# Transposing the residual by DMA instead of on TensorE, in a graph network with an LSTM

## The chip, the cores and the metric

The kernel runs on one core of a Trainium2 chip. The metric is device microseconds of that core for one execution, as the median of three runs.

## The reference

The input x has 32 batches of 256 nodes with 128 features. Four layers follow each other, each with a residual: `x = layernorm(x + layer(x))`. Layer 0 is a gated neighbour sum over the matrix adj. Layer 1 is a normalised neighbour sum, two dense layers (128 to 256 to 128), each with a batch norm over all 32 x 256 rows. Layer 2 is attention over the 256 nodes of a batch. Layer 3 is two neighbour sums with dense layers and then, for window lengths p = 1 to 4, an LSTM that runs p steps over windows of the nodes and writes its last state back. Cut to what matters here:

```python
x = _layernorm(x + _L0_gnn_ref(x, adj, ...), axis=-1)
x = _layernorm(x + _L1_gnn_ref(x, adj, ...), axis=-1)   # out = batchnorm(h @ W2.T + b2)
x = _layernorm(x + _L2_gnn_ref(x, adj, ...), axis=-1)
x = _layernorm(x + _L3_gnn_ref(x, adj, ...), axis=-1)
```

## The kernel before

The batches go in 8 groups of 4 (`GB`), so a group is 1024 rows of 128 features: 8 tiles of 128 x 128 (`TILES`; `COLS` = 1024). Everything is float32. Each engine has its own instruction queue, written out by hand, and the engines meet by semaphores.

The batch norms of layer 1 need all groups, so the kernel has two parts. The first does layer 0 and layer 1's matmuls for all groups. It leaves X1 (the sum after layer 0, normalised, with nodes on the partitions) and O2T (layer 1's output before its last batch norm, with features on the partitions) in SBUF. The second part goes in turns, `slot(s)` on each engine, for s = 2 to 10. In turn s four groups are in work at once: group s in stage A (end of layer 1, layer 2), group s - 1 in stage B (the matmuls of layer 3), group s - 2 in stage L (11 LSTM steps, `NSTEP`), group s - 3 in stage T (the last layernorm and the output). Groups 0 and 1 go through stage A ahead of the turns, in an order of their own. Stage A exists in turns 2 to 7, six times.

**The residual.** At the start of stage A the sum X1 + O2 is wanted with nodes on the partitions, and O2T has features there. GpSimd first scales and shifts O2T by the batch norm, two groups ahead (`scaled(s + 2)`, L504, semaphore yt_ok). TensorE then makes eight transposes into the PSUM tensor PA (`a_residual`, L680). VectorE adds X1 and writes Z (`a_sum1`, L1552, semaphore z1_ok). From Z come the row statistics (`a_norm1`, L1400), the dot products with two vectors (`a_dots`, L1570, 16 instructions, then `a_s12`, L1576) and ScalarE's normalised X2 (`norm_apply`, L1042).

**TensorE's order in a turn** is x(0), a_residual(s), x(1), t_turn, a_spread0 for two batches, x(2), a_spread0 for the other two, x(3), h(3), a_rows, a_weigh0, x(4), and on to step 10 with the attention's matmuls in between. x(k) and h(k) are the input and state matmuls of LSTM step k (L831, L843). The four gates have a PSUM bank each (`QQ`), so gate q of step k + 1 waits until ScalarE's tanh (L1200) has read gate q of step k.

**VectorE's order** is inner(0), a_sum1, state(0), inner(1), a_small2(s - 1), state(1), a_norm1, cell(2), t_sum (L1779), a_dots, a_s12, cell(3), a_max, cell(4) and so on. inner(k) (L1680, L1726 and others) makes the cell state, state(k) (L1708) the hidden state, cell(k) is both. x(2) waits for state(1), x(4) for state(3).

**GpSimd's order** in a turn is `rstd(1, 0, s)` (L446, L452), `scaled(s + 2)`, `tail(s - 3)` (L446 and L525, after step 6), then `rstd` and `scale2(s)` (L446, L512) for the two halves of group s. a_spread0(s) in the next turn waits for scale2. **SP's queue** has only DMAs: the loads, then the eight stores of a group's output as they become ready.

Of SBUF, the quarter `late[:, 2]` (2048 words of a partition) holds nothing in the turns.

Of the kernel before, what the change touches and what calls it, by code (L numbers as in the profile page):

```python
# [19 lines left out]

F32 = mybir.dt.float32
ACT = mybir.ActivationFunctionType
AX = mybir.AxisListType

P = 128
# [75 lines left out]
def build(nc, x, xt, adj, early_in, later_in, lstm_w, out):  # L101
    ctx = ExitStack()
    with ctx:
# [3 lines left out]
        def sem(name):  # L107
            return ctx.enter_context(nc.semaphore(name))
# [13 lines left out]
        MS, E1 = (late[:, k, :].rearrange("p (t n) -> p t n", n=NODES) for k in range(2))  # L122
        HS = late[:, 3, 0:2 * BANK].rearrange("p (k n) -> p k n", k=2)
        ZF = late[:, 3, 2 * BANK:4 * BANK]

        AN = late[:, 0, 0:BANK].rearrange("p (c n) -> p c n", c=NC)
        DIAG = late[:, 2, 0:NC * P].rearrange("p (c n) -> p c n", c=NC)
# [245 lines left out]
                  + [(i, h) for i in range(AHEAD, NCHUNK) for h in range(HC)])  # L373

        half_ps = sem("half_ps")

        lanes = [Lane(g_ps, g_ok, ca_ok, cf_ok, cell_ok, tc_ok, h_ok, Q, NGATE * LAST + GATE_AT[LANED, I],
                      FORGETS[NSTEP] * LAST, NSTEP * LAST + LANED),
# [13 lines left out]
        @block.sync  # L392
        def _(sp):
            def load_xt(g):
                sp.dma_start(XT[:, g % NX], xt[g]).then_inc(xt_in[g % NX], 16)

            def load_x(g):
                sp.dma_start(XIN[:, g % NX], x[g]).then_inc(x_in[g % NX], 16)

            sp.dma_start(AD[:, 1], adj[:, 1]).then_inc(adjt_in, 16)  # L400
            load_x(0)
            sp.dma_start(early[:], early_in).then_inc(early_ok, 16)
            load_xt(0)
            sp.dma_start(AD[:, 0], adj[:, 0]).then_inc(adj_in, 16)
            load_x(1)
            load_xt(1)
            load_x(2)
            load_xt(2)
            sp.dma_start(later[:], later_in).then_inc(later_ok, 16)
            load_xt(3)  # L410
            load_x(3)
            for g in range(NX, GROUPS):
                sp.wait_ge(gate_ps, g - NX + 1)
                load_xt(g)
                sp.wait_ge(mix3, g - NX + 1)
                load_x(g)
            sp.dma_start(WT[:], lstm_w).then_inc(lstm_in, 16)

            for g in range(GROUPS - 1):
                sp.wait_ge(ln[3]["out"], TILES * (g + 1))  # L420
                sp.dma_start(out[g], OUT[:, g % 2]).then_inc(sent[g % 2], 16)
            half = TILES // 2 * P
            sp.wait_ge(last_act, TILES // 2)
            sp.dma_start(out[GROUPS - 1][:, 0:half], OUT[:, 1, 0:half]).then_inc(sent[1], 16)
            sp.wait_ge(last_dve, LAST_DVE)
            sp.wait_ge(last_act, TILES - LAST_DVE)
            sp.dma_start(out[GROUPS - 1][:, half:], OUT[:, 1, half:]).then_inc(sent[1], 16)
            sp.wait_ge(sent[0], 16 * (GROUPS // 2))
            sp.wait_ge(sent[1], 16 * (GROUPS // 2 + 1))
# [3 lines left out]
        def _(pool):  # L433
# [66 lines left out]
            def scaled(g):  # L500
# [2 lines left out]
                o2 = O2T[:, g * COLS:(g + 1) * COLS]  # L503
                pool.tensor_scalar(o2, o2, BN[:, 4, 0:1], BN[:, 5, 0:1], ALU.mult, ALU.add).then_inc(yt_ok, 1)  # L504

            def scale2(g, h=None):
                f = front(g)
                pool.wait_ge(ln[2]["rstd"], halves(g, h))
# [19 lines left out]
            def slot(s, par, A, B, L, T):  # L528
                if A:
                    rstd(1, 0, s)  # L530
                    scaled(s + 2)
                if T:
                    tail(s - 3, 1 - par)
                if A:
                    for h in range(2):
                        rstd(2, 1, s, h)
                        scale2(s, h)
# [5 lines left out]
            rstd(1, 2, 1, 1)  # L543
            scaled(2)
            scaled(3)
            rstd(2, 1, 0, 0)
            scale2(0, 0)
            rstd(2, 1, 0, 1)
# [1 line left out]
            rstd(2, 2, 1, 0)  # L550
            rstd(2, 2, 1, 1)
            scale2(1)
            slots(slot)


        @block.tensor
        def _(pe):
# [113 lines left out]
                output1(i, h)  # L671


            def a_residual(g, h=None):
                pe.wait_ge(half_ok, 1) if (g, h) == (0, 1) else pe.wait_ge(yt_ok, g + 1)
                reach(pe, z2_ok, TILES * before(g))
                for b in batches(h):
                    for c in range(NC):
                        at = g * COLS + b * NODES + c * P
                        mm = pe.transpose(turned(front(g).PA, c, b), O2T[:, at:at + P], ident[:])  # L680
                mm.then_inc(y_ps, size(h))


            def a_preload(g, h):
                bs = slice(2 * h, 2 * h + 2)
                pe.matmul(front(g).PA[:, part(h)].rearrange("p (b c d) -> p b c d", c=NC, d=P), ident[:],
# [92 lines left out]


            def a_spread0(g, some, h=None):
                reach(pe, z1_ok, 2 * upto(g + 2) - 4)
                for b in some:
                    pe.wait_ge(ln[2]["out"], TILES * g + NC * (b + 1))
                    for m in range(NC):
# [109 lines left out]
            def slot(s, par, A, B, L, T):  # L895
# [47 lines left out]
                        h(k) if STEPS[k][1] else None  # L943
                    return
                x(0)
                a_residual(s) if A else None
                x(1)
                t_turn(s - 3, 1 - par) if T else None
                a_spread0(s - 1, (0, 1)) if B else None
# [391 lines left out]
        def _(dve):  # L1341
# [203 lines left out]
            o2 = O2T[:, 0:BANK]  # L1545
            dve.tensor_scalar(o2, o2, BN[:, 4, 0:1], BN[:, 5, 0:1], ALU.mult, ALU.add).then_inc(yt_ok, 1)

            def a_sum1(g, h=None):
                dve.wait_ge(y_ps, halves(g, h))
                f = front(g)  # L1550
                bs = slice(batches(h)[0], batches(h)[-1] + 1)
                dve.tensor_tensor(f.Z[:, part(h)].rearrange("p (b c d) -> p b c d", c=NC, d=P),  # L1552
                                  f.PA[:, part(h)].rearrange("p (b c d) -> p b c d", c=NC, d=P),
                                  X1[:, g, :].rearrange("p (c b d) -> p b c d", c=NC, d=P)[:, bs], ALU.add).then_inc(z1_ok, size(h))

            def a_norm1(g, h=None):
                if g < 2:
# [396 lines left out]
```

## Time and profile before

| what | us |
|---|---|
| median of 3 runs (lowest, highest) | 638.43 (638.06, 638.8) |
| span of the profiled execution | 636.4 |
| median of the runs less that span | 2.0 |
| TensorE busy, matmuls (share of the span) | 621.6 (98%) |
| VectorE busy | 474.8 (75%) |
| ScalarE busy | 433.8 (68%) |
| GpSimd busy | 167.4 (26%) |
| turns 2 to 7, start to start | 57.4 to 57.7 each |

The profile is of one execution. Its span runs from the first to the last instruction; no other time is recorded for that execution, so a sum is made against the span and carried to the runs with the 2.0 us between. PE is TensorE's matmul, PEld its weight load, DVE is VectorE, ACT is ScalarE, POOL is GpSimd, SP issues DMAs. L504 is line 504 of the kernel before. The rows name tensors by the first name of their memory: `HB` is also O2T, `raw` the LSTM's gates and cells, `four` the input, Z2 and output buffers, `one_a` to `one_d` work buffers.

### The profile page before, as it was taken

Reading aid. Unit: us, or ns where it says so; the run is one execution under the profiler, and the core shown is the slowest. Engines: PE = TensorE matmul, PEld = TensorE weight load, DVE = VectorE, ACT = ScalarE, POOL = GpSimd, SP = SyncE. Lnnn points to the kernel's source line nnn. Section 1 sums busy time; section 2 is a strip of 40 time slices with the busy share of each in tenths; the row PEclk is TensorE's granted clock in tenths of the full one; section 3 lists DMA queues with packets and bytes.
Section 4 is the critical chain, followed back from the end, with each engine's and each line's share of the span. In section 5 each row is a group of like instructions: output and inputs, shape, how many; then the busy total and the mean of one; then the engine's idle time right before and its main releaser. Section 6 shows DMA issues by size and latency. Waiting matters only on the chain.

```text
span 636.4 us, 9580 instructions
## 1 busy us (share of the span) xinstructions
PE 621.6 (98%) x2768; PEld 440.9 (69%) x2768; DVE 474.8 (75%) x1623; ACT 433.8 (68%) x995; POOL 167.4 (26%) x228
## 2 busy tenths in 40 slices
PE   9999999999999999999999999999999999999994
PEld 6756656447975687578658757865885687577794
DVE  4999999876847767866887787688768767465656
ACT  3667767966947766795677577557847766546774
POOL 1464551005233002304503240341143032103211
PEclk9999999999999999999999999999999999999998
DMA  8424000000000000000000000000000000000000
GB/s 337 142 115 166 1 1 1 1 0 2 2 1 1 0 2 0 2 2 33 2 0 2 34 1 2 33 2 1 1 33 2 2 28 6 1 1 33 2 35 33
DMA packets 4372, 16.84 MB, mean 26 GB/s; under 512 B 480, under 2 KB 480, under 8 KB 4192
## 3 DMA queue, kind: packets, MB, share of 16 engines
q1 hardware_dynamic: 4320, 16.23, 6.6%
q8 instruction: 22, 0.36, 0.2%
q14 instruction: 30, 0.25, 0.1%
HBM read 12.03 MB, written 4.19 MB: 26 GB/s over the span
## 4 chain that ended last, share of the span: by engine, by line
PE 76%; DVE 3%; ACT 2%; issue 1%; POOL 0%; POOLq 0%; ACTq 0%; DVEq 0%
PE QQ L831 26%; PE QQ L843 15%; PE PA L814 4%; PE PA L786 4%; PE PB L805 2%; PE PB L796 2%; PE PB L667 2%; PE PA L667 2%; PE PA L767 2%; PE PB L767 2%; PE QQ L865 1%; PE PB L884 1%; PE PB L746 1%; PE PA L746 1%; PE QQ L875 1%
## 5 line engine op out<-in xcount | busy, mean ns | idle before, releaser
L1200 ACT ACTIVATE raw<-QQ,BL 128x256 f32<-128x256 f32 (+2 forms) x279 | 150.1, 558 | 75.1 <-PE QQ L843 37.7
L831 PE MATMUL QQ<-HT,WT 128*128 128x256 f32 (+2 forms) x558 | 183.9, 474 | 1.1 <-ACT raw L1200 0.6
L446 POOL TENSOR_TENSOR RSD<-VAR,pw 128x4 f32<-128x4 f32 (+1 forms) x43 | 61.8, 1438 | 381.7 <-DVE VAR L1422 381.7
L831 PEld LDWEIGHTS QQ<-HT,WT 128*128 128x128 f32 x558 | 103.5, 190 | 59.2 <-issue 28.3
L843 PE MATMUL QQ<-HB,WT 128*128 128x256 f32 (+2 forms) x336 | 100.2, 441 | 0.4 <-DVE HB L1708 0.2
L843 PEld LDWEIGHTS QQ<-HB,WT 128*128 128x128 f32 x336 | 61.2, 190 | 29.3 <-issue 13.4
L1236 ACT ACTIVATE raw<-raw 128x256 f32<-128x256 f32 (+4 forms) x79 | 37.1, 470 | 25.9 <-DVE raw L1690 19.7
L1680 DVE SCALAR_TENSOR_TENSOR raw<-raw 128x256 f32<-128x256 f32 (+2 forms) x60 | 32.5, 542 | 20.2 <-ACT raw L1200 19.6
L1708 DVE SCALAR_TENSOR_TENSOR HB<-raw 128x256 f32<-128x256 f32 (+4 forms) x42 | 20.1, 478 | 23.5 <-ACT raw L1236 23.5
L1042 ACT ACTIVATE X<-Z,OFF,RSD 128x128 f32<-128x128 f32 x80 | 31.8, 482 | 2.0 <-POOL OFF L452 2.0
L512 POOL TENSOR_SCALAR X<-four,MEAN,RSD 128x128 f32<-128x128 f32 x64 | 30.7, 494 | 1.6
L622 PE MATMUL PA<-AHT,X 128*128 128x256 f32 x128 | 29.5, 384 | 1.5 <-ACT X L1042 1.3
L1163 ACT ACTIVATE HB<-HB,EB 128x256 f32<-128x256 f32 x64 | 30.9, 500 | 0.2
L786 PE MATMUL PA<-AD,X 128*128 128x256 f32 x128 | 30.3, 379 | 0.0
L622 PEld LDWEIGHTS PA<-AHT,X 128*128 128x128 f32 x128 | 23.7, 190 | 9.5 <-issue 6.3
L525 POOL TENSOR_SCALAR four<-HB,MEAN,RSD 128x128 f32<-128x128 f32 x56 | 29.7, 544 | 0.7
L636 PE MATMUL QQ<-one_b,later 128*128 128x512 f32 x64 | 29.1, 598 | 0.2 <-ACT one_b L1071 0.2
L814 PE MATMUL PA<-AD,Y 128*128 128x256 f32 x128 | 29.2, 380 | 0.0
L786 PEld LDWEIGHTS PA<-AD,X 128*128 128x128 f32 x128 | 23.9, 191 | 6.8 <-issue 4.1
L814 PEld LDWEIGHTS PA<-AD,Y 128*128 128x128 f32 x128 | 24.2, 190 | 4.2
L1083 ACT ACTIVATE HB<-QQ 128x512 f32<-128x512 f32 x32 | 17.9, 586 | 12.8 <-PE QQ L636 12.5
L599 PE MATMUL PB<-four,AD 128*128 128x512 f32 x56 | 25.7, 601 | 0.4 <-DMA four<-in_x 0.4
(249 smaller groups left out, 1177.5 us busy)
## 6 DMA issues: line engine op xcount, KB each, us to landing
four<-in_x SPq DMA_DIRECT2D x8, 512.0 KB, 4.0
raw<-in_xt SPq DMA_DIRECT2D x8, 512.0 KB, 6.5
out<-four SPq DMA_DIRECT2D x7, 512.0 KB, 2.6
WT<-in_lstm SPq DMA_DIRECT2D x1, 2048.0 KB, 8.0
later<-in_later SPq DMA_DIRECT2D x1, 725.5 KB, 10.3
AD<-in_adj SPq DMA_DIRECT2D x2, 256.0 KB, 4.8
out<-four SPq DMA_DIRECT2D x2, 256.0 KB, 2.0
early<-in_early SPq DMA_DIRECT2D x1, 275.0 KB, 4.5
```

What stands on the lines that cost most here:

```text
L446: pool.tensor_tensor(RSD[kk][:, ts], VAR[kk][:, ts], pw[:, ts], ALU.pow).then_inc(ln[k]["rstd"], some)
L512: pool.tensor_scalar(tile_of(X1, g, c, b), nth(f.Z2, t), MEAN[f.kk2][:, t:t + 1], RSD[f.kk2][:, t:t + 1], ALU.add, ALU.mult).then_inc(ln[2 ...
L622: mm = pe.matmul(PA[:, b * NODES:(b + 1) * NODES], tile_of(X1, g, m, b), AHT[:, m, :], start=(m == 0), stop=(m == NC - 1))
L786: mm = pe.matmul(PA[:, b * NODES:(b + 1) * NODES], tile_of(X1, g, m, b), ADJT[:, m, :], start=(m == 0), stop=(m == NC - 1))
L814: mm = pe.matmul(PA[:, b * NODES:(b + 1) * NODES], turned(Y, m, b), ADJT[:, m, :], start=(m == 0), stop=(m == NC - 1))
L831: mm = pe.matmul(steps_view(Q[q], k), WT[:, 0, (p - 1) * 4 + q, :], ht_view(par, k), start=True, stop=(s == 0))
L843: pe.matmul(Q[q][:, 0:nw * GB], WT[:, 1, (p - 1) * 4 + q, :], HS[:, (k - 1) % 2, 0:nw * GB], start=False, stop=True).then_inc(g_ps, 1)
L1042: act.activation(nth(to, t), nth(z, t), ACT.Identity, bias=OFF[kk][:, t:t + 1], scale=RSD[kk][:, t:t + 1]).then_inc(ln[k]["out"], 1)
L1163: e = act.activation(f.E1[:, t], f.E1[:, t], ACT.Exp, bias=f.EB[:, t:t + 1], scale=1.0, accum_out=DEN[:, t:t + 1] if g > 1 else None)
L1200: act.activation(TG[q][:, at:n], Q[q][:, at:n], ACT.Tanh, scale=0.5 if q == G else 0.25, bias=BL[:, p - 1, q:q + 1]).then_inc(g_ok, 1)
L1236: act.activation(TC[:, at:n], CELL[:, at:n], ACT.Tanh, scale=0.5).then_inc(tc_ok, 1)
L1680: dve.scalar_tensor_tensor(out=target[:, 0:n], in0=TG[I][:, 0:n], scalar=1.0, in1=TG[G][:, 0:n], op0=ALU.add, op1=ALU.mult).then_inc(cell_ ...
```

## The change

The eight transposes on TensorE go. In their place GpSimd, a turn ahead, copies group s + 1 of O2T, seen as 16-bit half-words, into two planes (low halves, high halves; `split`). SP issues one DMA transpose of the 128 x 2048 half-words, in 16 blocks of 128 columns (`turn_residual`). GpSimd weaves the two turned planes back into float32 words in Z (`merge`). VectorE's add then reads Z and X1 from SBUF and writes Z. The planes lie in `late[:, 2]`.

In turn s GpSimd does split(s + 1) and merge(s + 1) between scaled(s + 2) and tail(s - 3), for s = 2 to 6. For group 2, split(2) stands behind scaled(3), ahead of the turns, and merge(2) is GpSimd's last instruction before turn 2. merge(g) waits for the DMA, and for the readers of the Z before it (a_dots and ScalarE's norm_apply of group g - 1). a_spread0's wait for z1_ok becomes one for z2_ok of the group that it works on. Groups 0 and 1 are as before.

```diff
--- before.py
+++ after.py
@@ -19,6 +19,7 @@
 from concourse.alu_op_type import AluOpType as ALU
 
 F32 = mybir.dt.float32
+U16 = mybir.dt.uint16
 ACT = mybir.ActivationFunctionType
 AX = mybir.AxisListType
 
@@ -122,6 +123,7 @@
         MS, E1 = (late[:, k, :].rearrange("p (t n) -> p t n", n=NODES) for k in range(2))
         HS = late[:, 3, 0:2 * BANK].rearrange("p (k n) -> p k n", k=2)
         ZF = late[:, 3, 2 * BANK:4 * BANK]
+        PLAIN, TURNED = (late[:, 2, k * COLS:(k + 1) * COLS].bitcast(U16) for k in range(2))
 
         AN = late[:, 0, 0:BANK].rearrange("p (c n) -> p c n", c=NC)
         DIAG = late[:, 2, 0:NC * P].rearrange("p (c n) -> p c n", c=NC)
@@ -373,6 +375,7 @@
                   + [(i, h) for i in range(AHEAD, NCHUNK) for h in range(HC)])
 
         half_ps = sem("half_ps")
+        split_ok, turned_in, merged_ok = (sem(n) for n in ("split_ok", "turned_in", "merged_ok"))
 
         lanes = [Lane(g_ps, g_ok, ca_ok, cf_ok, cell_ok, tc_ok, h_ok, Q, NGATE * LAST + GATE_AT[LANED, I],
                       FORGETS[NSTEP] * LAST, NSTEP * LAST + LANED),
@@ -416,7 +419,15 @@
                 load_x(g)
             sp.dma_start(WT[:], lstm_w).then_inc(lstm_in, 16)
 
+            def turn_residual(g):
+                sp.wait_ge(split_ok, g - 1)
+                reach(sp, merged_ok, g - 2)
+                sp.dma_start_transpose(TURNED.rearrange("p (k n) -> p k n", n=P), PLAIN).then_inc(turned_in, 16)
+
+            turn_residual(2)
+            turn_residual(3)
             for g in range(GROUPS - 1):
+                turn_residual(g + 4) if g + 4 < GROUPS else None
                 sp.wait_ge(ln[3]["out"], TILES * (g + 1))
                 sp.dma_start(out[g], OUT[:, g % 2]).then_inc(sent[g % 2], 16)
             half = TILES // 2 * P
@@ -503,6 +514,21 @@
                 o2 = O2T[:, g * COLS:(g + 1) * COLS]
                 pool.tensor_scalar(o2, o2, BN[:, 4, 0:1], BN[:, 5, 0:1], ALU.mult, ALU.add).then_inc(yt_ok, 1)
 
+            def split(g):
+
+                pool.wait_ge(yt_ok, g + 1)
+                reach(pool, turned_in, 16 * (g - 2))
+                o2 = O2T[:, g * COLS:(g + 1) * COLS].bitcast(U16)
+                pool.tensor_copy(PLAIN.rearrange("p (k n) -> p k n", k=2), o2.rearrange("p (n k) -> p k n", k=2)).then_inc(split_ok, 1)
+
+            def merge(g):
+
+                pool.wait_ge(turned_in, 16 * (g - 1))
+                if g > 2:
+                    pool.wait_ge(dots_ok, 2 * TILES * (g - 2))
+                    pool.wait_ge(ln[1]["out"], TILES * g)
+                pool.tensor_copy(Z[:].bitcast(U16).rearrange("p (n k) -> p k n", k=2), TURNED.rearrange("p (k n) -> p k n", k=2)).then_inc(merged_ok, 1)
+
             def scale2(g, h=None):
                 f = front(g)
                 pool.wait_ge(ln[2]["rstd"], halves(g, h))
@@ -529,6 +555,8 @@
                 if A:
                     rstd(1, 0, s)
                     scaled(s + 2)
+                    split(s + 1) if s + 1 < GROUPS else None
+                    merge(s + 1) if s + 1 < GROUPS else None
                 if T:
                     tail(s - 3, 1 - par)
                 if A:
@@ -543,6 +571,7 @@
             rstd(1, 2, 1, 1)
             scaled(2)
             scaled(3)
+            split(2)
             rstd(2, 1, 0, 0)
             scale2(0, 0)
             rstd(2, 1, 0, 1)
@@ -550,6 +579,7 @@
             rstd(2, 2, 1, 0)
             rstd(2, 2, 1, 1)
             scale2(1)
+            merge(2)
             slots(slot)
 
 
@@ -671,16 +701,6 @@
                 output1(i, h)
 
 
-            def a_residual(g, h=None):
-                pe.wait_ge(half_ok, 1) if (g, h) == (0, 1) else pe.wait_ge(yt_ok, g + 1)
-                reach(pe, z2_ok, TILES * before(g))
-                for b in batches(h):
-                    for c in range(NC):
-                        at = g * COLS + b * NODES + c * P
-                        mm = pe.transpose(turned(front(g).PA, c, b), O2T[:, at:at + P], ident[:])
-                mm.then_inc(y_ps, size(h))
-
-
             def a_preload(g, h):
                 bs = slice(2 * h, 2 * h + 2)
                 pe.matmul(front(g).PA[:, part(h)].rearrange("p (b c d) -> p b c d", c=NC, d=P), ident[:],
@@ -779,7 +799,7 @@
 
 
             def a_spread0(g, some, h=None):
-                reach(pe, z1_ok, 2 * upto(g + 2) - 4)
+                pe.wait_ge(z2_ok, TILES * (g + 1)) if g else None
                 for b in some:
                     pe.wait_ge(ln[2]["out"], TILES * g + NC * (b + 1))
                     for m in range(NC):
@@ -943,7 +963,6 @@
                         h(k) if STEPS[k][1] else None
                     return
                 x(0)
-                a_residual(s) if A else None
                 x(1)
                 t_turn(s - 3, 1 - par) if T else None
                 a_spread0(s - 1, (0, 1)) if B else None
@@ -1545,13 +1564,10 @@
             o2 = O2T[:, 0:BANK]
             dve.tensor_scalar(o2, o2, BN[:, 4, 0:1], BN[:, 5, 0:1], ALU.mult, ALU.add).then_inc(yt_ok, 1)
 
-            def a_sum1(g, h=None):
-                dve.wait_ge(y_ps, halves(g, h))
-                f = front(g)
-                bs = slice(batches(h)[0], batches(h)[-1] + 1)
-                dve.tensor_tensor(f.Z[:, part(h)].rearrange("p (b c d) -> p b c d", c=NC, d=P),
-                                  f.PA[:, part(h)].rearrange("p (b c d) -> p b c d", c=NC, d=P),
-                                  X1[:, g, :].rearrange("p (c b d) -> p b c d", c=NC, d=P)[:, bs], ALU.add).then_inc(z1_ok, size(h))
+            def a_sum1(g):
+                dve.wait_ge(merged_ok, g - 1)
+                z = Z[:].rearrange("p (b c d) -> p b c d", c=NC, d=P)
+                dve.tensor_tensor(z, z, X1[:, g, :].rearrange("p (c b d) -> p b c d", c=NC, d=P), ALU.add).then_inc(z1_ok, 2)
 
             def a_norm1(g, h=None):
                 if g < 2:
```

## Rows read from the trace of the kernel before

**Rows 1.** Busy time by stretch, turn 4: length, then each engine's busy us and instructions.

```profile
core 0: us, PE busy (x) PEld busy (x) DVE busy (x) ACT busy (x) POOL busy (x), PEclk, DMA share, GB/s
...
302.85:360.34 57.49, 57.49 (x251) 41.45 (x251) 44.08 (x154) 40.38 (x91) 15.69 (x23) 1.00 0.03 10
```

**Rows 2.** Timeline, all engines, start of turn 4: start us, us, what, idle before and releaser.

```profile
304.99 0.42 ACT L1236 ACTIVATE raw<-raw 128x256 f32<-128x256 f32 x1 [2.08 <-DVE raw L1690]
305.26 1.04 PE L680 MATMUL PA<-ident,HB 128*128 128x128 f32 x8
305.32 1.83 ACT L1200 ACTIVATE raw<-QQ,BL 128x512 f32<-128x512 f32 x3
...
306.14 2.32 PE L831 MATMUL QQ<-HT,WT 128*128 128x512 f32 x5
```

**Rows 3.** Timeline, all engines, x(2) of turn 4.

```profile
310.62 0.69 DVE L1708 SCALAR_TENSOR_TENSOR HT<-raw 128x512 f32<-128x512 f32 x1
...
311.36 0.19 PEld L831 LDWEIGHTS QQ<-HT,WT 128*128 128x128 f32 x1 [0.21 <-DVE HT L1708]
```

**Rows 4.** Timeline of GpSimd, turn 4.

```profile
316.78 1.20 POOL L504 TENSOR_SCALAR HB<-HB,BN 128x1024 f32<-128x1024 f32 x1
344.56 1.75 POOL L446 TENSOR_TENSOR RSD<-VAR,pw 128x8 f32<-128x8 f32 x1 [26.59 <-DVE VAR L1422]
...
358.92 1.01 POOL L446 TENSOR_TENSOR RSD<-VAR,pw 128x4 f32<-128x4 f32 x1 [8.30 <-DVE VAR L1422]
```

**Rows 5.** Timeline of VectorE, turn 4, from t_sum to step 3.

```profile
316.31 1.22 DVE L1779 SCALAR_TENSOR_TENSOR HB<-PB,X 128x1024 f32<-128x1024 f32 x1
317.44 0.68 DVE L1570 CUSTOM_DVE_ANT_0 one_a<-Z,WAR 128x128 f32<-128x128 f32 x1
...
318.04 0.28 DVE L1570 CUSTOM_DVE_ANT_0 one_a<-Z,WAR 128x128 f32<-128x128 f32 x1
...
321.84 0.69 DVE L1726 SCALAR_TENSOR_TENSOR raw<-raw 128x512 f32<-128x512 f32 x1 [0.33 <-ACT raw L1200]
```

**Rows 6.** Timeline, all engines, a_dots of turn 2.

```profile
201.72 1.49 POOL L504 TENSOR_SCALAR HB<-HB,BN 128x1024 f32<-128x1024 f32 x1
...
202.24 1.11 DVE L1570 CUSTOM_DVE_ANT_0 one_a<-Z,WAR 128x128 f32<-128x128 f32 x1
```

**Rows 7.** Timeline, all engines, start of turn 2.

```profile
188.72 3.88 POOL L512 TENSOR_SCALAR X<-four,MEAN,RSD 128x128 f32<-128x128 f32 x8
...
191.80 1.23 DVE L1552 TENSOR_TENSOR Z<-PA,X 128x1024 f32<-128x1024 f32 x1 [0.37 <-PE PA L680]
...
194.17 0.69 DVE L1680 SCALAR_TENSOR_TENSOR raw<-raw 128x512 f32<-128x512 f32 x1 [0.55 <-ACT raw L1200]
...
196.37 1.13 PE L831 MATMUL QQ<-HT,WT 128*128 128x512 f32 x2 [0.37 <-DVE HT L1708]
```

**Rows 8.** Groups by line and shape, whole span: busy us, mean ns of one.

```profile
L478 POOL TENSOR_TENSOR one_d<-one_d,Y 128x512 f32<-128x512 f32 x6 | 7.9, 1340 | 10.9 <-ACT one_d L1056 10.9
...
L1452 DVE SCALAR_TENSOR_TENSOR X<-X,four 128x1024 f32<-128x1024 f32 x4 | 4.9, 1224 | 0.1
```

**Rows 9.** Line L504: shortest, median and longest ns, first and last start.

```profile
L504 POOL TENSOR_SCALAR HB<-HB,BN x7: 1193/1195/1492, 145.0 to 374.3; 128x1024 f32<-128x1024 f32 x7
```

**Rows 10.** Timeline of GpSimd, ahead of the turns.

```profile
169.65 1.01 POOL L446 TENSOR_TENSOR RSD<-VAR,pw 128x4 f32<-128x4 f32 x1 [12.93 <-DVE VAR L1422]
```

**Rows 11.** Timeline, all engines, x(4) of turn 4.

```profile
325.02 0.40 PEld L831 LDWEIGHTS QQ<-HT,WT 128*128 128x128 f32 x2 [0.45 <-DVE HT L1708]
...
325.23 0.45 PE L831 MATMUL QQ<-HT,WT 128*128 128x340 f32 x1
```

**Rows 12.** Timeline of VectorE, step 3 in turn 2 and in turn 6.

```profile
206.85 0.69 DVE L1726 SCALAR_TENSOR_TENSOR raw<-raw 128x512 f32<-128x512 f32 x1 [1.15 <-ACT raw L1200]
...
436.83 0.69 DVE L1726 SCALAR_TENSOR_TENSOR raw<-raw 128x512 f32<-128x512 f32 x1 [0.71 <-ACT raw L1200]
```

**Rows 13.** DMA issues: count, KB each, median us from issue to landing.

```profile
out<-four SPq DMA_DIRECT2D x7, 512.0 KB, 2.6
```

## The prediction

> **What bounds the kernel now.** I read the busy time by stretch first. Turns 2 to 7, in which the changed code runs, last about 57.5 us each, and in turn 4 TensorE is busy for all of it [rows 1]. That invites the reading that eight matmuls less are eight matmuls saved. So I went on to the timeline of one turn's start, to see not whether TensorE is busy but what would let it begin the next matmul sooner. In turn 4 the queue is x(0), the residual, x(1), t_turn, half of a_spread0, x(2). x(1) begins at 306.14 [rows 2]. It overwrites the bank of gate I, so it waits for ScalarE's tanh of x(0)'s gate I. That tanh starts at 305.32 in a run of three (1.83 us, about 0.6 each and 0.69 for one alone), so it ends at about 306.0 [rows 2]. It cannot start sooner: before it in ScalarE's order stands the last tanh of the turn before (304.99), which had waited 2.08 us for VectorE [rows 2]. One step on, x(2)'s weights are loaded at 311.36, after a wait on VectorE's L1708, which runs from 310.62 for 0.69 us [rows 3]. So the residual fills a hole: TensorE is full, but the LSTM chain through ScalarE and VectorE arrives at the same moment to within 0.1 us, twice.
>
> Then the two engines that get work. GpSimd is idle for most of a turn: it ends L504 at 317.98 and is wanted again at 344.56 and 358.92 [rows 4]. VectorE is the one to watch, since some of its instructions stop while GpSimd runs [rows 5, 6].
>
> **The change, part by part.**
>
> *Removed: eight transposes a turn.* In turn 4 from 305.26 to 306.14, 0.88 us [rows 2], so 5.3 us in six turns if all of it counted. By the paragraph above x(1) can come up by about 0.1 us and x(2) by less than 0.1. In the five full turns (3 to 7) the gain is 0 to 0.4 us together; I take 0. In turn 2 x(1) would come up by the whole 0.88, but there another wait decides, next.
>
> *VectorE's add.* a_sum1 read PSUM and X1 and now reads Z and X1: 1.23 us before [rows 7], 1.22 for an add of the same size with both inputs in SBUF [rows 8]. No change. Its new wait, merged_ok, is met long before in turns 3 to 7.
>
> *merge(2) ahead of turn 2.* It stands on GpSimd behind scale2(1), eight instructions from 188.72 that end at 192.60 [rows 7]. Before, a_sum1(2) began at 191.80. Now it waits for the whole merge. Behind it on VectorE stand state(0), inner(1) and state(1), for which x(2) waits.
> The price of a copy: no row shows one of 2048 half-words. Nearest is L504, 1024 elements in 1.195 us when undisturbed [rows 9]; an instruction that it locked out (below) lost 0.83 us, which is the part that grows with length, so twice the elements cost 1.195 + 0.83 = 2.05 us. Lower bound: 1.2, if two half-words pass as one word. Upper bound: 5.2, four times the 1.3 us of a two-input operation on 512 elements [rows 8].
> With 2.05 and 0.1 to start, merge ends at 194.75 and a_sum1 starts 3.0 late. inner(1) had 0.55 us of waiting on ScalarE in front of it [rows 7], which absorbs that much: x(2) comes at about 198.8 instead of 196.37, **2.4 us late**, in place of the 0.88 gained. split(2) and its transfer lie earlier, in a gap of GpSimd of 12.9 us before 169.65 [rows 10], and have until 192.6: nothing.
>
> *split in turns 2 to 6.* It runs behind rstd and scaled, while VectorE does a_dots. In turn 2 L504 ran from 201.72 to 203.21, and the a_dots instruction that started at 202.24 took 1.11 us [rows 6] against 0.28 [rows 5]. In turn 4 the first a_dots takes 0.68 and is over when L504 is [rows 4, 5]. L1779, which has one input in PSUM, ran beside L504 in its usual 1.22 [rows 4, 5]. So two-SBUF-input instructions of VectorE stand still while GpSimd streams, 0.83 us for 1024 elements, 1.7 for split's 2048.
> The Trainium skill, "SBUF — State Buffer", section "SBUF: two separate sides", has this as an exclusive lock held for the whole instruction; by that 2.05 would be lost to a copy and not 1.7, and the sum would be some 3 us higher.
> What is late next: a_dots, then L1726 of step 3, which has 0.33 us of slack (its wait on ScalarE) [rows 5], then h for x(4): L1708's release at 325.02, the matmul at 325.23, 0.2 of slack [rows 11]. So x(4) is late by 1.7 - 0.33 - 0.2 = 1.2 us in turns 3, 4 and 5: **3.6**. In turn 2 L1726 had 1.15 of slack and in turn 6 0.71 [rows 12]: 0.35, and about 0.7 as there is no scaled ahead of it there: **1.0**. TensorE has no idle time in which to win it back.
>
> *The transfer.* 512 KB within SBUF. The nearest row, 512 KB to HBM, lands after 2.6 us [rows 13]: lower bound. Upper bound: sixteen blocks one behind the other at that price, 42 us. A transpose in half-words should be slower than a copy, but much nearer to one DMA than to sixteen: I take 3 to 8. SP's queue holds only out[g] behind it; tail needs that buffer two turns on.
>
> *merge in turns 2 to 6.* split ends near 320.4, so merge starts at 323 to 328, and it too stops VectorE for 1.7 us. Until 326.3 (step 3, shifted) VectorE does two-SBUF work on which x(4) waits; then a_max, one input in PSUM, leaves some 2.7 us free; then step 4. A merge costs 0 to 1.7; as most of the stretch is exposed I take 0.9, five times: **4.5**. tail and scale2 come at 344.56 and 358.92, too late to be touched.
>
> Sum: 2.4 + 3.6 + 1.0 + 4.5 = 11.5 us on the span of 636.4, so 647.9. The timed runs' median is 638.43, 2.0 above the span; with that, 650.
>
> **The rivals.**
>
> *TensorE's queue is the bound and moves up.* If x(1) and x(2) follow TensorE alone, each turn loses 0.88: 638.4 - 5.3 = 633. For it: 57.49 us busy of 57.49 [rows 1]. Against it: the two releases within 0.1 us [rows 2, 3]. It decides where turn 2's wait and all the locks stay below 5.3 us together. 6 in 100.
>
> *The copies are slow.* At 5.2 us, with about 4.8 held: turn 2 loses 5.5, the splits 4.3 x 3 + 3.5 + 3.9, the merges half of 4.8 five times, together 38: 676. For it: GpSimd at two inputs [rows 8]. Against it: L504 at one input [rows 9]. 20 in 100.
>
> *The copies are fast.* At 1.2 us, 0.83 held: 1.5 in turn 2, 0.3 three times, merges mostly in a_max: 641. 8 in 100.
>
> *The blocks move one after another at a microsecond or so each.* 16 to 24 us: merge falls at 337 to 345, where VectorE has several gaps and GpSimd nothing to do until 344.56 [rows 4]; the merges then cost nearly nothing, 645. 10 in 100.
> The Trainium skill, "VectorE: DVE Perf Modes", section "The three transpose paths", gives 1309 ns for one 128x128 block of two-byte elements by DMA; sixteen in a row would be 21 us (an estimate from that page), which leads to this case. No run here shows it.
>
> *The transfer outlasts the turn.* From about 30 us on, the merge holds tail, and behind it rstd and scale2, for which a_spread0 waits. At 42 us: split(2)'s merge 8 us later than in the sum, GpSimd some 6 us late in each of turns 3 to 7: 685. 6 in 100.
>
> **How the numbers follow.** The forecast, 645 to 656, has 50 in 100. A measurement of this kernel tells no change from one within 0.2%, 1.3 us. Faster gets the first rival's 6; 4 for the case that its gain and the losses cancel come out of the forecast's and the fast copies' lower ends; 90 for slower. For 8 in 10 I leave out the first rival, the long transfer and the upper half of the slow copies: 641 to 674.
>
> **What would show each step.** Right: in turns 3 to 7 a new wait of TensorE at x(1) on ScalarE, about 0.8 us, with x(2) where it was relative to x(0); in turn 2 a_sum1 waiting on GpSimd and x(2) some 2.4 us late; an a_dots instruction of about 2 us in turns 2 to 6; GpSimd's copies at 2.05 us; turns of 59 to 60 us. Wrong: turns of 56.6 us (first rival), copies of 4 us or more, merges that start past 330, or full-length copies beside undisturbed a_dots. A lock that doesn't hold for half-words would take 8 us out of the sum.

## The result, and the profile after

The changed kernel takes **660.12 us** (median of 4 runs, 659.04 to 661.56) against 638.26 for the kernel before, run beside it: a ratio of 1.0342 [1.0326, 1.0358], 22 us slower. The profiled execution's span is 659.0 us against 636.4, +22.6. The sum that the prediction made of its own steps was +11.5. The sign was right and the range, 641 to 674, holds the time, but the forecast, 650 with its own range 645 to 656, is too low by half of the loss. Nearly all that follows asks where the other 11 us are. The four executions spread over 2.5 us, those of the kernel before over 0.7.

The busy time by stretch, of the kernel after, for turns 2 to 7 (columns as in [rows 1]: length, then busy us and instructions of PE, PEld, DVE, ACT, POOL, then granted clock, DMA share, GB/s):

```profile
187.88:251.61 63.73, 57.85 (x235) 40.29 (x236) 40.54 (x123) 39.67 (x89) 16.28 (x17) 0.97 0.05 9
251.61:313.59 61.98, 58.84 (x244) 41.32 (x243) 47.65 (x154) 40.26 (x91) 20.48 (x25) 0.97 0.07 18
313.59:374.46 60.87, 57.42 (x244) 40.36 (x243) 47.81 (x154) 40.39 (x91) 20.18 (x25) 1.00 0.07 18
374.46:436.69 62.23, 58.84 (x244) 41.38 (x243) 47.87 (x154) 40.27 (x91) 20.16 (x25) 0.97 0.07 18
436.69:497.93 61.24, 58.64 (x245) 41.39 (x244) 46.95 (x154) 40.29 (x91) 18.83 (x24) 0.97 0.07 18
497.93:555.42 57.49, 56.87 (x244) 40.51 (x243) 43.69 (x154) 40.38 (x91) 14.51 (x22) 1.00 0.03 10
```

Before, turn 2 took 57.19 us and each of the others 57.5 (x(0) began at 188.00, 245.19, 302.69 and so on). So the turns lose 6.5, 4.5, 3.4, 4.7, 3.7 and 0.0 us, 22.8 together: the whole loss. Turn 7, in which there is nothing left to split or merge, is back at 57.49. Turns 3, 4 and 5 do the same work and don't lose the same, and the column that tells turn 4 from the other two is the granted clock.

TensorE's waits in the kernel after, the two groups that grew most (us in total, times, longest). Before, the wait of x(2) for L1708, now L1724, was 0.37 us in turn 2 [rows 7]:

```profile
PE QQ L851 <- DVE HT L1724: 14.8, 6, 4.0
PE QQ L851 <- ACT raw L1219: 3.4, 6, 0.6
```

The timeline of the kernel after, first at the start of turn 2, then two rows of turn 3, x(1) and x(4), and then turn 4 (start, us, what, idle before and releaser). L538 is scale2, L522 split, L530 merge; L851 is x(k), L1570 a_sum1, L1586 a_dots, L1742 to L1754 step 3's inner(3), L1603 a_max. The 14 matmuls of 340 columns are those of x(4) and x(5), which follow each other:

```profile
188.58 3.88 POOL L538 TENSOR_SCALAR X<-four,MEAN,RSD 128x128 f32<-128x128 f32 x8
...
192.42 2.48 POOL L530 COPY Z<-HB 128x2048 uint16<-128x2048 uint16 x1
...
195.00 1.23 DVE L1570 TENSOR_TENSOR Z<-Z,X 128x1024 f32<-128x1024 f32 x1 [3.71 <-POOL Z L530]
...
198.97 4.43 PE L851 MATMUL QQ<-HT,WT 128*128 128x512 f32 x6 [3.97 <-DVE HT L1724]
...
254.70 2.84 PE L851 MATMUL QQ<-HT,WT 128*128 128x512 f32 x6 [0.36 <-ACT raw L1219]
...
277.05 5.96 PE L851 MATMUL QQ<-HT,WT 128*128 128x340 f32 x14 [2.33 <-DVE HT L1724]
...
313.59 2.74 PE L851 MATMUL QQ<-HT,WT 128*128 128x512 f32 x6
...
316.95 2.84 PE L851 MATMUL QQ<-HT,WT 128*128 128x512 f32 x6 [0.62 <-ACT raw L1219]
...
322.31 2.81 PE L851 MATMUL QQ<-HT,WT 128*128 128x512 f32 x6
...
328.83 1.94 POOL L522 COPY HB<-HB 128x2048 uint16<-128x2048 uint16 x1
...
328.95 1.96 DVE L1586 CUSTOM_DVE_ANT_0 one_a<-Z,WAR 128x128 f32<-128x128 f32 x1
...
330.80 1.84 SPq L425 DMA_TRANSPOSE HB<-HB  x1
...
330.85 0.28 DVE L1586 CUSTOM_DVE_ANT_0 one_a<-Z,WAR 128x128 f32<-128x128 f32 x1
...
334.63 0.75 DVE L1748 SCALAR_TENSOR_TENSOR raw<-raw 128x256 f32<-128x256 f32 x2
...
335.11 2.60 POOL L530 COPY Z<-HB 128x2048 uint16<-128x2048 uint16 x1 [4.33 <-DMA HB<-HB]
335.30 2.97 DVE L1754 SCALAR_TENSOR_TENSOR raw<-raw 128x256 f32<-128x256 f32 x2
...
339.16 0.42 DVE L1603 CUSTOM_DVE_ANT_0 HB<-PA,NEG 128x256 f32<-128x256 f32 x1
339.30 4.27 PE L851 MATMUL QQ<-HT,WT 128*128 128x340 f32 x14 [2.33 <-DVE HT L1724]
```

**Start of a turn** (answers to [rows 2, 3]). x(1) now waits 0.62 us for ScalarE and begins 3.36 after x(0), against 3.45 before; x(2) begins 8.72 after x(0), against 8.71. The 0.88 us of transposes went, and a wait stands in their place. Turns 5 to 7 are the same. In turn 3 x(1) waits 0.36 us and turn 3's start is 0.27 us shorter; what goes with that is in the run moved_all.

**Start of turn 2** (answers to [rows 7]). scale2 as before, then the merge, then a_sum1 after a wait of 3.71 on it; x(2) at 198.97 instead of 196.37, 2.6 late (2.7 counted from x(0), which begins 0.12 sooner here). Its six matmuls take 4.43 us where they took 2.84, as this row of the kernel before shows:

```profile
196.37 2.84 PE L831 MATMUL QQ<-HT,WT 128*128 128x512 f32 x6 [0.37 <-DVE HT L1708]
```

**The split** (answers to [rows 4 to 6]). It runs from 328.83 for 1.94 us and holds one a_dots for 1.96; the next one takes 0.28, as before [rows 5]. So 1.68 us of the 1.94 are lost on VectorE. The a_dots began 0.12 us after split and ended 0.14 us after it, so it was held for all that was left of split. The Trainium skill, "SBUF — State Buffer", section "SBUF: two separate sides", has an exclusive lock between two-SBUF-input instructions and GpSimd, which is held for the whole instruction. The trace agrees, at 0.14 us. L504 held an a_dots in the same way in the kernel before: in turn 2 it ended at 203.21 and the a_dots beside it at 203.35 [rows 6], again 0.14 later. What an a_dots loses is thus the rest of GpSimd's instruction less 0.14 us, and not a share of its length: 1.82 - 0.14 for split, 0.97 - 0.14 for L504. In turn 6 split runs from 450.75 to 452.64 and the a_dots beside it begins only at 451.45; it loses 1.06.

**The merge.** The transfer's landing releases it at 335.11, 4.3 us after SP issues. Between lie the other 14 a_dots, a_s12, L1742 and L1748. L1748, just ahead of the merge, takes 0.75 for a pair; L1754, of the same shape, takes 2.97 for a pair. That is 2.2 us lost on the chain to x(4), ahead of a_max, which starts at 339.16. x(4), which had 0.2 us to spare [rows 11], waits 2.33.

**Clock.** Two levels are to be seen, 2.4 GHz (1.00) and 1.2 GHz: in the kernel after the granted clock is 0.50 from 198.97 to 200.50 and 1.00 from 202.30 to 203.30. A stretch of 0.6 to 0.7 has some of both. In windows of the kernel after:

```profile
198.97:203.30 4.33, 4.33 (x7) 1.95 (x8) 2.37 (x14) 1.37 (x2) 1.50 (x1) 0.63 0.01 4
277.05:282.85 5.80, 5.80 (x14) 3.65 (x15) 4.40 (x19) 2.80 (x6) 0.00 (x0) 0.71 0.00 0
339.30:345.00 5.70, 5.65 (x19) 3.58 (x20) 4.99 (x21) 3.42 (x7) 0.00 (x0) 1.00 0.00 0
400.00:406.00 6.00, 5.84 (x15) 3.76 (x16) 4.48 (x20) 2.80 (x6) 0.00 (x0) 0.72 0.00 0
461.00:467.00 6.00, 5.62 (x14) 3.54 (x15) 4.59 (x20) 2.80 (x6) 0.00 (x0) 0.72 0.00 1
```

Each stretch begins with the matmul for which TensorE waited, or up to 0.4 us ahead of it: 3.97 us ahead of the first, 2.33, 2.33, 2.33 and 1.98 ahead of the others. In turns 3, 5 and 6 the 14 matmuls of x(4) and x(5) then take 5.96 us and in turn 4, at full clock, 4.27. In turn 2 x(4) waited 1.85 us, and its 14 matmuls took 4.27 at a clock of 1.00.

The copies, in the groups by line with busy us and mean ns (answer to [rows 8, 9]), and the transfer, in the DMA issues with the median from issue to landing (answers to [rows 13]):

```profile
L530 POOL COPY Z<-HB 128x2048 uint16<-128x2048 uint16 x6 | 15.4, 2561 | 21.7 <-DMA HB<-HB 21.7
...
L522 POOL COPY HB<-HB 128x2048 uint16<-128x2048 uint16 x6 | 11.9, 1990 | 0.0
```

```profile
HB<-HB SPq DMA_TRANSPOSE x6, 4.3
```

### The profile page after: what moved, and what is told of

Its sections match the earlier page's. It is cut to its first block, busy times and chain, and to the rows that moved or that the text cites. A ratio compares the mean times of both kernels' runs of the same rounds, so it can differ in the third digit from the quotient of the medians.

```text
span 659.0 us, 9511 instructions
## 1 busy us (share of the span) xinstructions
PE 625.5 (95%) x2720; PEld 438.1 (66%) x2720; DVE 493.5 (75%) x1623; ACT 433.3 (66%) x995; POOL 194.1 (29%) x240
## 4 chain that ended last, share of the span: by engine, by line
PE 56%; DVE 17%; ACT 5%; issue 5%; POOL 1%; DVEq 0%; ACTq 0%; POOLq 0%
PE QQ L851 17%; PE QQ L863 12%; PE PA L834 4%; DVE one_a L1586 3%; PE PB L825 2%; DVE STL L1419 2%; PE PB L697 2%; PE PA L697 2%; DVE raw L1696 2%; PE PA L806 2%; PE PB L787 2%; PE PA L787 2%; DVE raw L1754 1%; ACT raw L1219 1%; DVE HT L1724 1%
## 5 line engine op out<-in xcount | busy, mean ns | idle before, releaser
L851 PE MATMUL QQ<-HT,WT 128*128 128x256 f32 (+2 forms) x558 | 191.4, 489 | 18.4 <-DVE HT L1724 14.8
L851 PEld LDWEIGHTS QQ<-HT,WT 128*128 128x128 f32 x558 | 106.5, 196 | 86.2 <-issue 33.8
L1724 DVE SCALAR_TENSOR_TENSOR HB<-raw 128x256 f32<-128x256 f32 (+4 forms) x42 | 20.4, 486 | 24.8 <-ACT raw L1255 24.8
L538 POOL TENSOR_SCALAR X<-four,MEAN,RSD 128x128 f32<-128x128 f32 x64 | 31.1, 499 | 1.6
L652 PEld LDWEIGHTS PA<-AHT,X 128*128 128x128 f32 x128 | 23.7, 190 | 9.5 <-issue 6.4
```

Of the source, the lines that this page charges most:

```text
L538: pool.tensor_scalar(tile_of(X1, g, c, b), nth(f.Z2, t), MEAN[f.kk2][:, t:t + 1], RSD[f.kk2][:, t:t + 1], ALU.add, ALU.mult).then_inc(ln[2 ...
L652: mm = pe.matmul(PA[:, b * NODES:(b + 1) * NODES], tile_of(X1, g, m, b), AHT[:, m, :], start=(m == 0), stop=(m == NC - 1))
L851: mm = pe.matmul(steps_view(Q[q], k), WT[:, 0, (p - 1) * 4 + q, :], ht_view(par, k), start=True, stop=(s == 0))
```

## The experiments

The theory from this profile: no gain from the removal, 2.6 us for turn 2's wait, about 3.4 us a turn for the two locks, and the rest from falls of the clock that follow TensorE's waits. Rivals: that the DMA's traffic slows the engines; that TensorE's queue would have moved up if nothing else stood in the way; that the lower clock is only an effect of the idle time and costs nothing by itself.

### no_transposes: the removal alone

Before, with `a_residual` taken out of TensorE's order and a_sum1 reading SBUF (a_spread0's wait is changed as in the kernel after):

```diff
-                a_residual(s) if A else None
...
-            def a_sum1(g, h=None):
-                dve.wait_ge(y_ps, halves(g, h))
+            def a_sum1(g):
+                dve.wait_ge(ln[1]["out"], TILES * g)
+                z = Z[:].rearrange("p (b c d) -> p b c d", c=NC, d=P)
+                dve.tensor_tensor(z, X2[:].rearrange("p (b c d) -> p b c d", c=NC, d=P),
+                                  X1[:, g, :].rearrange("p (c b d) -> p b c d", c=NC, d=P), ALU.add).then_inc(z1_ok, 2)
```

> The kernel before, with the eight transposes of each turn taken out and nothing in their place: the add sums X1 and the X2 of the group before, both in SBUF, so layer 1's part is missing from groups 2 to 7. If the LSTM chain sets the start of x(1) and x(2), as the prediction says: turns 3 to 7 keep 57.5 us to within 0.1, turn 2 loses some 0.9 us of its start, 637 to 638 us in all. If TensorE's queue is the bound: every turn 0.88 us shorter, 633.

637.48 us (636.94 to 638.04), 0.9989 [0.998, 0.9998]. The timeline of TensorE in its turn 4:

```profile
301.64 2.74 PE L831 MATMUL QQ<-HT,WT 128*128 128x512 f32 x6
305.00 1.98 PE L831 MATMUL QQ<-HT,WT 128*128 128x512 f32 x4 [0.62 <-ACT raw L1199]
```

The same 0.62 us as in the kernel after, and turns 3 to 7 of 57.50 us, unchanged. Turn 2 alone is shorter, 56.33 instead of 57.19: there nothing else held x(1). So what the removal itself is worth, with no cost beside it, is 0.7 to 0.9 us. The rival of 633 is false.

### dma_alone: the six DMA transposes beside the kernel before

The transposes read and write the empty quarter `late[:, 2]`, with no copies. In turn 4 the transfer is issued 13.8 us after x(0) (in the kernel after 17.2), and so beside a_dots, as there:

```diff
+            def turn_residual(g):
+                sp.wait_ge(yt_ok, 3) if g == 2 else sp.wait_ge(ln[1]["rstd"], 2 * g)
+                reach(sp, turned_in, 16 * (g - 2))
+                sp.dma_start_transpose(TURNED.rearrange("p (k n) -> p k n", n=P), PLAIN).then_inc(turned_in, 16)
...
+                turn_residual(g + 4) if g + 4 < GROUPS else None
```

> The kernel before, with the six DMA transposes added and issued at the same places of a turn, their result unused; no copies on GpSimd, the residual stays on TensorE. If the loss of the change comes from GpSimd's copies: no change, 638 us to within 0.7, and no instruction of VectorE or TensorE longer beside the transfer. If the transfer of 256-byte pieces slows the engines' access to SBUF: a good part of the 22 us, 643 or more.

638.57 us, 1.0003 [0.9994, 1.0011], and 4.3 us to landing as in the kernel after. The traffic costs nothing that this measurement can tell. The Trainium skill, "SBUF — State Buffer", section "SBUF: two separate sides", says that engines and DMAs have ports of their own; this run, at 1.0003, agrees.

### merge2_early: turn 2's wait taken away

```diff
+            merge(2)
             ...
-            merge(2)
```

merge(2) goes from behind GpSimd's last work for group 1 to a place ahead of it; the rest is the kernel after.

> The changed kernel, with the copy back for group 2 put ahead of the last rstd and scale2 before the turns, where GpSimd has 10 us of idle time. If that copy alone holds the start of turn 2: the add waits for nothing, x(2) comes 2.6 us earlier, and the stretch behind it at the lower granted clock (0.63 from 198.97 to 203.30, some 1.6 us) goes too: 656 us. If x(2) were held by something else as well: 659 to 660.

654.94 us, 1.0267 [1.0253, 1.0281]; 5.2 less than after. Its timeline:

```profile
191.49 1.21 DVE L1570 TENSOR_TENSOR Z<-Z,X 128x1024 f32<-128x1024 f32 x1
...
195.67 2.84 PE L851 MATMUL QQ<-HT,WT 128*128 128x512 f32 x6 [0.41 <-DVE HT L1724]
```

a_sum1 doesn't wait, x(2) is back, and its matmuls take 2.84 again, with a clock of 1.00 from 199 to 204. Turn 2 falls from 63.73 to 58.83, by 4.9, more than the 2.6 by which x(2) was late. From x(0) to x(2) are 7.52 us here, 11.09 in the kernel after and 8.37 before, so x(2) gains 3.6: its whole lateness and the 0.85 that the removal is worth in this turn, as in no_transposes. The rest, 1.3, is the clock's. Of turns 3 to 5 it is now turn 4 that is longer, 62.25, and the two others are alike, 60.86: the wait at x(4) is 2.33 us in turn 4 and 2.32 in turn 3, and the 14 matmuls then take 5.96 at a clock of 0.71 in the one and 4.27 at 1.00 in the other.

### kept_busy: all waits left, the clock held up

The kernel after, with matmuls of the constant ones into a free bank while TensorE waits: 17 ahead of x(2) in turn 2, and 10 ahead of x(4) in turns 2 to 6. Nobody reads what they write.

```diff
+                spin(Q[F][:, 0:P], 17) if s == 2 else None
...
+                if s < LAST:
+                    pe.wait_ge(g_ok, NGATE * (s - 2) + GATE_AT[3, F] + 1)
+                    spin(Q[F][:, 0:P], 10)
```

> The changed kernel, with matmuls of ones into the free bank of gate F while TensorE would wait: 17 ahead of x(2) in turn 2, 10 ahead of x(4) in turns 2 to 6. The waits themselves stay. If the fall of the granted clock behind those waits (0.63 to 0.72 in four stretches of the changed kernel's profile) is a cost of its own: the clock stays at 1.00 and about 1.5 us come back four times, 654 us. If the locks and the wait are all there is: 660, as the changed kernel.

655.8 us (655.68 to 655.87), 1.0275 [1.0261, 1.0289]; 4.3 less than after, with more matmuls. The timeline of TensorE, turn 2 and turn 4 (320.07 is x(2), 343.77 x(6)):

```profile
195.00 3.96 PE L591 MATMUL QQ<-ones 128*128 128x128 f32 x34
199.14 2.84 PE L851 MATMUL QQ<-HT,WT 128*128 128x512 f32 x6 [0.18 <-DVE HT L1728]
...
320.07 2.81 PE L851 MATMUL QQ<-HT,WT 128*128 128x512 f32 x6
...
334.57 2.40 PE L591 MATMUL QQ<-ones 128*128 128x128 f32 x20
337.07 4.27 PE L851 MATMUL QQ<-HT,WT 128*128 128x340 f32 x14
...
343.77 2.45 PE L851 MATMUL QQ<-HT,WT 128*128 128x340 f32 x8
```

x(2) in turn 2 and x(4) in turn 4 come as late as in the kernel after, 11.09 us behind x(0) and 17.0 behind x(2), but at full clock. Its turns 2 to 7 take 62.42, 60.88, 60.88, 60.87, 59.85 and 57.50: the three like turns are now alike, each 3.38 above 57.5. So 3.38 is the price of the two locks in turns 3 to 5, and 2.35 in turn 6. From x(2) to x(6) turns 3, 5 and 6 of the kernel after take 1.4 us more each, and its turn 2 is 1.3 longer: that is the clock's. The rival by which the clock costs nothing of its own is false. The profiled execution is 5.0 us shorter than that of the kernel after, the medians differ by 4.3: the four executions lie within 0.2 us here and within 2.5 there, where the granted clock of the whole execution goes from 0.986 to 0.991. That suggests that the executions of the kernel after differ in their falls; only one was profiled.

### merges_moved: the locks told apart

The kernel after, with the merges of turns 2 to 6 behind tail, where they wait for the attention's transposes (semaphore pt_ok); the splits stay.

```diff
-                    merge(s + 1) if s + 1 < GROUPS else None
...
+                if A and s + 1 < GROUPS:
+                    pool.wait_ge(pt_ok, GB * (s - 1) + 3)
+                    merge(s + 1)
```

> The changed kernel, with the copy back of turns 2 to 6 held until VectorE's third copy of attention weights (pt_ok), behind tail: there VectorE reads PSUM for some 4 us. split, and the late copy for group 2, stay. If the lock sets the price: step 3 loses only split's part, x(4) is late by about 1.2 us instead of 3.2 in turns 3 to 5 and by 0.3 in turns 2 and 6, and the fall of the clock behind x(4) goes: 13 us less than the changed kernel, 647 us. If a copy costs the same wherever it stands: 660.

645.3 us (644.81 to 647.62), 1.0117 [1.0101, 1.0134]. Turns 2 to 7 are 61.60, 58.39, 58.67, 58.39, 57.37 and 57.51. Turns 3, 5 and 6 have a start that is 0.27 us shorter, with a wait of 0.35 us at x(1) instead of 0.62 (more on it below); behind x(2) turns 3 and 5 are like turn 4. In turn 4 x(2) and x(6) stand at:

```profile
317.18 2.81 PE L853 MATMUL QQ<-HT,WT 128*128 128x512 f32 x6
...
338.68 2.45 PE L853 MATMUL QQ<-HT,WT 128*128 128x340 f32 x8
```

From x(2) to x(6) are 21.50 us, against 20.32 in the kernel before (311.40 to 331.72) and 23.70 in kept_busy. So split costs 1.2 us and the merge 2.2, and so it is in turns 3 and 5. In turn 6 split costs 0.1 and the merge 2.2. In turn 2 the merge's place is worth 2.1 against the kernel after. The falls of the clock behind x(4) have gone with the merges: the list of waits has none at x(4) any more, the granted clock is 1.00 in turns 3 to 7, and only turn 2's fall, after the wait of 4.0 us that is still there, remains.

### moved_all: every copy moved to where it hides

merge(2) early, the merges behind tail, and the splits where they wait for the first a_max (semaphore max_ok):

```diff
-                    split(s + 1) if s + 1 < GROUPS else None
-                    merge(s + 1) if s + 1 < GROUPS else None
+                    if s + 1 < GROUPS:
+                        pool.wait_ge(max_ok, TILES * s + 1)
+                        split(s + 1)
```

> The changed kernel, with all its copies where VectorE reads PSUM or GpSimd is idle: group 2's copy back ahead of the last rstd before the turns, split behind the first a_max of a turn, the copy back as in the run with moved copies back. The DMA transposes stay. If waits and locks are the whole loss: TensorE waits only at x(1), the turns are 57.5 us, 637.5 as in the run without transposes. If half-words, DMA transposes or the longer GpSimd work cost something of their own: 640 or more.

**636.41 us** (635.68 to 636.67), 0.9968 [0.9956, 0.998]: 1.9 us faster than the kernel before and 23.7 faster than the kernel after, with the same copies and transfers. Its timeline of GpSimd and VectorE, from the start of turn 4 to the start of turn 5 (L538 is scale2, L522 split, L530 merge, L1607 a_max, L1706 cell work of step 10):

```profile
301.67 2.16 POOL L538 TENSOR_SCALAR X<-four,MEAN,RSD 128x128 f32<-128x128 f32 x4
...
302.92 0.59 DVE L1706 SCALAR_TENSOR_TENSOR raw<-raw 128x256 f32<-128x256 f32 x1
...
324.52 1.89 POOL L522 COPY HB<-HB 128x2048 uint16<-128x2048 uint16 x1 [7.36 <-DVE MX L1607]
...
324.71 0.42 DVE L1607 CUSTOM_DVE_ANT_0 HB<-PA,NEG 128x256 f32<-128x256 f32 x1
...
350.12 2.49 POOL L530 COPY Z<-HB 128x2048 uint16<-128x2048 uint16 x1 [0.35 <-DVE HB L1628]
...
359.18 2.47 POOL L538 TENSOR_SCALAR X<-four,MEAN,RSD 128x128 f32<-128x128 f32 x4
...
360.39 0.42 DVE L1706 SCALAR_TENSOR_TENSOR raw<-raw 128x256 f32<-128x256 f32 x1
```

a_max has one input in PSUM. Its instructions take 0.42 us each beside the split, as in the kernel after, where nothing runs beside it: here there is no lock to pay for. Turns 3 to 6 are 1.17, 1.15, 1.16 and 0.14 us shorter than in merges_moved, in which only the splits and merge(2) stand elsewhere; that is split's price once more.

Of the 1.9 us, 0.9 is turn 2 (56.33 us). Turn 4 takes 57.52, as before, but turns 3 and 5 to 7 take 57.23. The place is x(1)'s wait, 0.35 us there and 0.62 in turn 4. At the start of turn 5 scale2 takes 2.47 us instead of 2.16, and L1706 takes 0.42 instead of 0.59. GpSimd waits for VectorE there, and not the other way round; the cell ahead of ScalarE's tanh of x(0) is not held, and the tanh comes earlier. The two go together in turns 3 to 7 of every run read here that waits at x(1): with 0.35 or 0.36 us at x(1) scale2 takes 2.47 to 2.49, with 0.61 to 0.63 it takes 2.16. So it is in turn 3 of the kernel after and in turns 3, 5 and 6 of merges_moved. Why it falls one way or the other, no run here shows.

### filled_pe and filled: can the hole at x(1) be used?

filled_pe is moved_all with a_spread0's first batch between x(0) and x(1). filled also puts a_sum1 behind state(1) in VectorE's order, so that x(2) would be released sooner.

```diff
+                a_spread0(s - 1, (0,)) if B else None
...
-                a_spread0(s - 1, (0, 1)) if B else None
+                a_spread0(s - 1, (1,)) if B else None
```

```diff
-                a_sum1(s) if A else None
...
+                a_sum1(s) if A else None
```

> As the run with all copies moved, and on TensorE one batch of a_spread0 (0.86 us) goes from behind t_turn into the hole between x(0) and x(1). If x(2) is held by VectorE's state(1) as well: TensorE waits at x(2) instead of at x(1), same time, 637 to 638. If the hole at x(1) were all that keeps the 0.88 us of a turn from counting: 633.

> As that run, and on VectorE a_sum1 goes from between inner(0) and state(0) to behind state(1), which a residual that is ready a turn ahead allows. If the LSTM chain through state(1) holds x(2): x(2) comes some 0.4 us earlier in each of six turns, 635 to 636, faster than both kernels. If x(2) is held by ScalarE's tanhs alone: 637.5.

filled_pe: 637.58 us, 0.9987 [0.9978, 0.9996], 1.2 more than moved_all. TensorE's wait moves one step on, to x(2) (its timeline, turn 4):

```profile
302.91 2.74 PE L855 MATMUL QQ<-HT,WT 128*128 128x512 f32 x6
...
306.35 2.74 PE L855 MATMUL QQ<-HT,WT 128*128 128x512 f32 x6
...
311.32 1.98 PE L855 MATMUL QQ<-HT,WT 128*128 128x512 f32 x4 [0.41 <-DVE HT L1729]
```

x(2) comes 8.41 us after x(0). scale2 takes 2.47 us in this turn; in the turns of moved_all in which it does, x(2) came 8.45 after x(0). So the filled hole brings 0.04 us. In turn 2, where x(1) had no wait and so no hole, x(2) comes 0.85 later than in moved_all and the turn takes 57.17 us instead of 56.33, which is most of the 1.2.

filled: 640.08 us (639.32 to 640.61), 1.0026 [1.0016, 1.0036], where 635 to 636, or else 637.5, was expected: a miss both ways. x(2) comes 8.70 after x(0) in turn 4 (303.59 to 312.29), in which scale2 takes 2.16 us, and 8.42 in turns 3 and 6, in which it takes 2.47, as in filled_pe. So a_sum1 was not what held it. By the timeline ScalarE's tanhs were: two runs of three, and a tanh of the cell between them 0.2 us after the first (its timeline, turn 4; x(2) waits for the state behind the second run's cell):

```profile
306.24 1.83 ACT L1224 ACTIVATE raw<-QQ,BL 128x512 f32<-128x512 f32 x3
...
308.27 0.63 ACT L1260 ACTIVATE raw<-raw 128x512 f32<-128x512 f32 x1 [0.20 <-DVE raw L1701]
...
308.80 1.83 ACT L1224 ACTIVATE raw<-QQ,BL 128x512 f32<-128x512 f32 x3
```

a_sum1, now later, delays what follows instead: in turn 4 x(6) comes 20.84 us after x(2), in moved_all 20.33, and the turns grow to between 57.5 and 58.0. So in these runs the start of a turn is bound by the LSTM's chain over ScalarE and VectorE, whatever TensorE has in between. moved_all stays the best version found.

## Why the prediction was right, and where it was short

The direction was right and for the reasons given: nothing gained by the removal, a late x(2) in turn 2, and locks on the chain to x(4). That the range 641 to 674 holds the 660 owes something to luck. The forecast's own part ended at 656; what lies above it stood there for slow copies, and the copies were not slow.

- **The removal gains nothing: right.** 0 was taken in turns 3 to 7, and x(1)'s new wait of 0.62 us (0.36 in turn 3) stands where the transposes were; 0.8 was foretold. In no_transposes those turns don't change at all. The two releases within 0.1 us [rows 2, 3] told this; the 57.49 us of busy TensorE [rows 1] would have told 633.
- **Turn 2's wait: right.** 2.4 predicted, 2.6 measured. merge(2) was a little longer (2.48 for 2.05).
- **Prices of the copies and the transfer: right in kind.** 2.05 predicted, 1.99 for split and 2.56 for merge; 4.3 us for the transfer within 3 to 8. The rivals of slow copies, fast copies, blocks one after another and a transfer that outlasts the turn fall with them. The Trainium skill, "VectorE: DVE Perf Modes", section "The three transpose paths", gives 1309 ns for one block. Sixteen of them in a row would be 21 us, an estimate from that page. The trace has another price for blocks of one instruction: all sixteen land in 4.3 us.
- **split's lock: right in size, in part by luck.** 1.7 predicted, 1.68 measured; 1.2 late in turns 3 to 5 predicted, 1.2 measured. But the 0.83 us that L504 cost an a_dots was not the part of L504 that grows with length, doubled for split and added for a copy's price. It was what was left of L504 when that a_dots began, 0.97 us, less 0.14. That twice this number comes near split's 1.68 is chance, and so is the 2.05 for a copy of 1.89 undisturbed. Turn 6 shows it: the a_dots begins 0.7 us into split, loses 1.06 instead of 1.7, and the turn loses 0.1 us where about 0.7 was taken.
- **merge's lock: the term that was mis-sized.** The step that failed reads "A merge costs 0 to 1.7; as most of the stretch is exposed I take 0.9, five times". It costs 2.2 in turns 3 to 6, and in turn 2 the two locks cost 2.5 together: some 11 us instead of 4.5. Two things were wrong. The lock is longer, 2.2 us, as the merge is 2.6 long. And a mean over the stretch was taken where there is no spread: the transfer takes 4.3 us in each turn, and what VectorE does in the meantime is fixed too, so the merge falls on step 3's inner(3) every time. With the landing time worked out (split's end, plus the transfer, against 14 a_dots of 0.21 us, a_s12 and L1742) the place could have been found for any assumed transfer. An estimate from turn 4's rows: step 3 ends with L1724 at 339.25 (338.83 for 0.42), so without the merge at about 337.0. A merge that starts before that falls on work for which x(4) waits, and all transfers below about 6 us of the 3 to 8 do that.
- **The clock: a term that was missing.** The prediction let a wait of TensorE cost its own length. Four of the six longer waits were followed by a stretch at a granted clock of 0.63 to 0.72, which cost 1.3 us in turn 2 and 1.4 in turns 3, 5 and 6: 5.5 in all. kept_busy gave back 4.3 by the medians with every wait in place.
- **Two sums of the prediction are off.** A lock that doesn't hold for half-words would take 3.6 + 1.0 + 4.5 = 9 us out of its sum, not 8, and the terms of the 42 us transfer add up to about 683, not 685. Neither changes the forecast.

Measured terms: 2.7 for turn 2's wait, 2.5 for its two locks, 3.6 for split and 8.8 for merge in turns 3 to 6, 5.5 for the clock, less 0.3 for turn 3's shorter start: 22.8 together, as the six turns lose. Where the sum went by rows of VectorE it was near, if partly by chance; what it lacked was the place in time of one instruction and what TensorE does after a wait.

## What to carry to other kernels

When an engine off the critical path is given work, ask where in the other engines' order it falls, and place it there: the same copies cost over 20 us in one place, and behind a_max and tail nothing that the turns show. An instruction whose start is set by a transfer of constant length falls on the same victim in each round, so work out the victim instead of a mean. When an engine is held by another's long instruction, what it loses is what is left of that instruction, so the price depends on where the two starts lie and not on the length alone. A wait of TensorE of 2 to 4 us cost its length and in four cases of six 1.3 to 1.4 us more in clock; matmuls that nobody reads, put into the wait, won most of that part back.

## What the runs showed of the hardware

- A DMA transpose of 128 x 2048 half-words within SBUF took 4.3 us from issue to landing (median of six), and six of them beside a full kernel changed its time by nothing (1.0003 [0.9994, 1.0011]).
- GpSimd's half-word copies of 128 x 2048 took 1.89 us where they gather strided halves into planes undisturbed, and 2.5 to 2.6 where they weave planes into strided halves.
- Two-input VectorE instructions in SBUF lost 1.68 us to a split of 1.94 and 2.2 to a merge of 2.6; a_max, with one input in PSUM, lost nothing to a whole split. An a_dots that scaled or split held ended 0.12 to 0.15 us after GpSimd's instruction, in the kernels before and after alike, whether 0.5 or 1.8 us of it had been left.
- In the kernel after, waits of the same 2.33 us at the same place were followed by a fall of the clock in turns 3 and 5 and by none in turn 4; in merge2_early turn 4 is the long one. What decides it, no run here shows.
